# Normalizing the merged heads: four ACTIVATEs on ScalarE in place of four tensor_scalars on VectorE

## The chip, the cores and the metric

One Trainium2 chip, one core. The metric is the device time of one execution in microseconds. The profile shows the engines TensorE (PE, with its weight loads PEld), VectorE (DVE), ScalarE (ACT), GpSimd (POOL) and SyncE (SP), which here only issues transfers.

## The reference, cut to what matters

4096 tokens of width 256 go through two layers: attention in blocks, a mixture of experts, a recurrent token mixer with a channel mixer, and a second mixture of experts, each followed by a layer norm without weights. The step of this document is the first of these norms:

```python
def _layernorm(x, axis=-1, eps=1e-05):
    m = jnp.mean(x, axis=axis, keepdims=True)
    v = jnp.var(x, axis=axis, keepdims=True)
    return (x - m) / jnp.sqrt(v + eps)

x = L0_attn_hidden_states
x = _layernorm(x + _L0_attn_ref(x, ...), axis=-1)
x = _layernorm(x + _L0_ffn_ref(x, ...), axis=-1)
...
```

The attention leaves, in DRAM, the context of all 16 heads not yet divided by the sums of the softmax, and those sums. Merging the heads means: divide each head's context by its sum, add the layer's input, normalize each token's row.

## The kernel before

The program is a chain of stages, and each ends with a barrier of all engines. `merge_heads` is the third, after `project_qkv` and `attend`; `route` follows. It works on `NGRP` = 8 groups of `GRP` = 512 tokens, each as `GT` = 4 tiles of 128 rows by 256 columns, with two buffers (`s = g % 2`) for nearly everything. For a group:

- SyncE loads the contexts `c`, the sums `z` and the layer's input `hidden` (`load`, L823 to L825).
- TensorE (`bring`, L849 and L850) transposes contexts and sums of a tile into the PSUM bank `ps[j]`. It waits for all three loads of the group, and per tile for the bank.
- VectorE (`divide`, L868 and L873) takes the reciprocal of the sums and multiplies.
- GpSimd (L897) adds `hidden` and writes `x`. It waits until the group two before is normalized, whose buffer it takes.
- VectorE (`Norm.stats`, L748 and L752) takes mean and variance of each row.
- ScalarE (`Norm.root`, L761) takes the square root of the variance plus epsilon.
- VectorE (`Norm.apply`, L765 and L773) takes its reciprocal and, tile by tile, writes `y` = (x - mean) * inverse. Each tile counts up the semaphore `normed`.
- SyncE (`Norm.store`, L795) stores `y` to DRAM, once `normed` has the whole group.
- TensorE (`Norm.turn`, L783) transposes `y`, 8 blocks into two banks, and ScalarE (`Norm.copy`, L790) copies both banks to `xT`, on which `route` works.

The class `Norm` is used by two stages, `merge_heads` and `mix_channels`, each with tiles of its own name (`merge_...`, `mlp_...`). The last stage, `last_norm` (tiles `combine_...`), is code of its own: there ScalarE does the normalizing, with a scale and a bias per row.

Each engine runs its list in order, and the order within a step g is what matters here:

```python
sync:    load(g + 2)       # after added(g);   then  store(g)  after normed(g)
tensor:  bring(g + 1);     turn(g - 1)
vector:  divide(g + 1);    apply(g);    stats(g + 1)
gpsimd:  add of group g
scalar:  root(g);          copy(g - 1)
```

So the loads of group g + 3 stand behind the store of group g in SyncE's list, and the turn of group g - 1 behind the whole of `bring(g + 1)` in TensorE's.

Of the kernel before, what the change touches and what calls it, by code (L numbers as in the profile page):

```python
# [9 lines left out]
ALU = mybir.AluOpType  # L10
ACT = mybir.ActivationFunctionType
AX = mybir.AxisListType

P = 128
T = 4096
D = 256
KD = D // P
# [3 lines left out]
GT = GRP // P  # L21
# [18 lines left out]
class Mem:  # L40


    def __init__(self, nc, ctx, tag):
        self.nc, self.ctx, self.tag = nc, ctx, tag
# [18 lines left out]
def token_rows(a, g):  # L63

    return a[bass.ds(g * GRP, GRP), :].rearrange("(j p) d -> p j d", p=P)
# [640 lines left out]
def beyond(g, n):  # L706

    return not isinstance(g, int) or g > n


def skewed(first, last, step):


    for g in range(first, NGRP + last):
        step(g, g % 2)


def exists(g):

    return not isinstance(g, int) or 0 <= g < NGRP  # L720


class Norm:
# [3 lines left out]
    def __init__(self, nc, m, x, ready, out_d, ident=None, xT=None, also=()):  # L727
        self.outs = (out_d, *also)
        self.nc, self.x, self.ready, self.ident, self.xT = nc, x, ready, ident, xT
        self.y = [m.sb(f"y{i}", [P, GT, D]) for i in range(2)]  # L730
        self.part = [m.sb(f"part{i}", [P, GT, 6]) for i in range(2)]
        self.mean_var = [m.sb(f"mean_var{i}", [P, GT, 2]) for i in range(2)]
        self.std = [m.sb(f"std{i}", [P, GT]) for i in range(2)]
        self.inv = [m.sb(f"inv{i}", [P, GT]) for i in range(2)]
        self.eps = m.sb("eps", [P, 1])
        self.bank = [m.ps(f"turn{k}", [P, GRP]) for k in range(KD)] if xT is not None else None
        self.eps_set, self.parted, self.aggregated, self.std_done, self.inv_done, self.normed = (
            m.sem(a) for a in ("eps_set", "parted", "aggregated", "std_done", "inv_done", "normed"))
        self.turned, self.copied, self.passed = m.sem("turned"), m.sem("copied"), m.sem("ln_passed")
        self.stored = [m.sem(f"stored{i}") for i in range(2)]  # L740
# [22 lines left out]
    def apply(self, dve, g, s):  # L763
        dve.wait_ge(self.std_done, g + 1)
        self.nc.vector.reciprocal(self.inv[s][:, :], self.std[s][:, :]).then_inc(self.inv_done, 1)  # L765
        if beyond(g, 1):

            dve.wait_ge(self.stored[s], 16 * len(self.outs) * (g // 2))
            if self.xT is not None:
                dve.wait_ge(self.turned, KD * (g - 1))  # L770
        dve.wait_ge(self.inv_done, g + 1)
        for j in range(GT):
            self.nc.vector.tensor_scalar(self.y[s][:, j, :], self.x[g % len(self.x)][:, j, :], self.mean_var[s][:, j, 0:1],  # L773
                                         self.inv[s][:, j:j + 1], ALU.subtract, ALU.mult).then_inc(self.normed, 1)

    def turn(self, pe, g, s):
        pe.wait_ge(self.normed, GT * (g + 1))
        for k in range(KD):
            if beyond(g, 0):

                pe.wait_ge(self.copied, KD * (g - 1) + k + 1)
            for j in range(GT):
                mm = self.nc.tensor.transpose(self.bank[k][:, j * P:(j + 1) * P], self.y[s][:, j, k * P:(k + 1) * P],  # L783
                                              self.ident[:, :])
            mm.then_inc(self.turned, 1)
# [16 lines left out]
def merge_heads(nc, hs, ctx_d, sums_d, ident, out_d, xT):  # L802


    with ExitStack() as ctx:
        m = Mem(nc, ctx, "merge")
        c = [m.sb(f"c{i}", [P, KD, GRP]) for i in range(2)]
        z = [m.sb(f"z{i}", [H, GRP]) for i in range(2)]
        hidden = [m.sb(f"hidden{i}", [P, GT, D]) for i in range(2)]
        x = [m.sb(f"x{i}", [P, GT, D]) for i in range(2)]  # L810
        inv = [m.sb(f"inv_sum{i}", [P, H]) for i in range(2)]
        scaled = [m.sb(f"scaled{i}", [P, D]) for i in range(4)]
        ps = [m.ps(f"ps{i}", [P, 512]) for i in range(4)]
        in_ = [m.sem(f"in{i}") for i in range(2)]
        brought, inverted, multiplied, added = m.sem("brought"), m.sem("inverted"), m.sem("multiplied"), m.sem("added")
        norm = Norm(nc, m, x, added, out_d, ident, xT)
        block = ctx.enter_context(nc.Block())

        @block.sync
        def _(sp):  # L820
            def load(g, s):
                toks = bass.ds(g * GRP, GRP)
                sp.dma_start(c[s][:, :, :], ctx_d.rearrange("(k p) t -> p k t", p=P)[:, :, toks]).then_inc(in_[s], 16)  # L823
                sp.dma_start(z[s][:, :], sums_d[:, toks]).then_inc(in_[s], 16)
                sp.dma_start(hidden[s][:, :, :], token_rows(hs, g)).then_inc(in_[s], 16)  # L825

            def step(g, s):
                if exists(g + 2):
                    if beyond(g, -1):

                        sp.wait_ge(added, GT * (g + 1))
                    load(g + 2, s)
                if exists(g):
                    norm.store(sp, g, s)

            skewed(-2, 0, step)
            norm.finish(sp)

        @block.tensor
        def _(pe):  # L840
            def bring(g, s):
                pe.wait_ge(in_[s], 48 * (g // 2 + 1))
                for j in range(GT):
                    if beyond(g, 0):

                        pe.wait_ge(multiplied, GT * (g - 1) + j + 1)
                    cols = slice(j * P, (j + 1) * P)
                    for k in range(KD):
                        nc.tensor.transpose(ps[j][:, k * P:(k + 1) * P], c[s][:, k, cols], ident[:, :])  # L849
                    nc.tensor.transpose(ps[j][:, D:D + H], z[s][:, cols], ident[0:H, 0:H]).then_inc(brought, 1)  # L850

            def step(g, s):
                if exists(g + 1):
                    bring(g + 1, 1 - s)
                if exists(g - 1):
                    norm.turn(pe, g - 1, 1 - s)

            skewed(-1, 1, step)

        @block.vector  # L860
        def _(dve):
            norm.begin()

            def divide(g, s):
                for j in range(GT):
                    n = GT * g + j
                    dve.wait_ge(brought, n + 1)
                    nc.vector.reciprocal(inv[j % 2][:, :], ps[j][:, D:D + H]).then_inc(inverted, 1)  # L868
                    if beyond(g, 0):

                        dve.wait_ge(added, n - GT + 1)
                    dve.wait_ge(inverted, n + 1)
                    nc.vector.tensor_tensor(  # L873
                        scaled[j][:, :].rearrange("p (h d) -> p h d", h=H),
                        ps[j][:, 0:D].rearrange("p (h d) -> p h d", h=H),
                        inv[j % 2][:, :].rearrange("p (h a) -> p h a", a=1).broadcast_to([P, H, HD]),
                        ALU.mult).then_inc(multiplied, 1)

            def step(g, s):
                if exists(g + 1):  # L880
                    divide(g + 1, 1 - s)
                if exists(g):
                    norm.apply(dve, g, s)
                if exists(g + 1):
                    norm.stats(dve, g + 1, 1 - s)

            skewed(-1, 0, step)

        @block.gpsimd
        def _(pool):  # L890
            def step(g, s):
                if beyond(g, 1):

                    pool.wait_ge(norm.normed, GT * (g - 1))
                for j in range(GT):
                    pool.wait_ge(multiplied, GT * g + j + 1)
                    nc.gpsimd.tensor_tensor(x[s][:, j, :], scaled[j][:, :], hidden[s][:, j, :], ALU.add).then_inc(added, 1)  # L897

            skewed(0, 0, step)

        @block.scalar
        def _(act):
            def step(g, s):
                if exists(g):
                    norm.root(act, g, s)
                if exists(g - 1):
                    norm.copy(act, g - 1, 1 - s)

            skewed(0, 1, step)

# [1668 lines left out]
```

## Time and profile before

| | |
|---|---|
| median of 3 runs | 2062.33 us (2059.09 to 2065.66) |
| profiled execution, time | 2058.43 us |
| profiled execution, span | 2056.7 us |
| merge stage, first load to the first transfer of `route` | 661.46 to 725.86 us of the span |

The profile is of one execution. Times within it are microseconds from the start of its span. "Idle before" in a row of a timeline is how long the engine stood idle before this instruction, and what ended that. A transfer's row (SPq) is its issue; when it has landed is seen from who waited for it.

### The profile page before, as it was taken

Reading aid. Unit: us, or ns where it says so; the run is one execution under the profiler, and the core shown is the slowest. Engines: PE = TensorE matmul, PEld = TensorE weight load, DVE = VectorE, ACT = ScalarE, POOL = GpSimd, SP = SyncE. Lnnn points to the kernel's source line nnn. Section 1 sums busy time; section 2 is a strip of 40 time slices with the busy share of each in tenths; the row PEclk is TensorE's granted clock in tenths of the full one; section 3 lists DMA queues with packets and bytes.
Section 4 is the critical chain, followed back from the end, with each engine's and each line's share of the span. In section 5 each row is a group of like instructions: output and inputs, shape, how many; then the busy total and the mean of one; then the engine's idle time right before and its main releaser. Section 6 shows DMA issues by size and latency. Waiting matters only on the chain. (4 is left out here: it accounts for less than half of the span.)

```text
span 2056.7 us, 34775 instructions
## 1 busy us (share of the span) xinstructions
PE 1729.3 (84%) x12738; PEld 1378.9 (67%) x12738; DVE 1191.2 (58%) x2624; ACT 879.6 (43%) x1734; POOL 642.5 (31%) x644
## 2 busy tenths in 40 slices
PE   5859999999995778799888838969997479999991
PEld 4625766666674457767666634538997379999991
DVE  4657677777751857564443426756765755566643
ACT  2300666666675254352222216645443043444433
POOL 1340011111121467755555531113331023323111
PEclk9955799999998588899999978989999589999996
DMA  5794133333311661123333321010111322343314
GB/s 193 261 150 60 48 70 74 80 74 86 80 19 47 197 238 69 73 47 56 57 56 52 52 57 53 19 44 1 62 42 62 123 39 79 90 136 94 79 14 165
DMA packets 140644, 169.57 MB, mean 82 GB/s; under 512 B 72170, under 2 KB 108480, under 8 KB 140480
## 3 DMA queue, kind: packets, MB, share of 16 engines
q1 hardware_dynamic: 101248, 111.86, 18.5%
q0 software_dynamic: 32128, 51.82, 12.1%
q10 hardware_dynamic: 7104, 3.67, 1.3%
q8 instruction: 107, 1.75, 0.4%
q14 instruction: 57, 0.47, 0.1%
HBM read 109.20 MB, written 61.34 MB: 83 GB/s over the span
## 5 line engine op out<-in xcount | busy, mean ns | idle before, releaser
L583 DVE TENSOR_REDUCE att_neg_max<-att_m_ps 128x1 f32<-128x320 f32 x496 | 235.1, 487 | 131.4 <-PE att_m_ps L410 123.6
L410 PE MATMUL att_m_ps<-att_k,att_q 96*128 96x384 f32 x496 | 230.0, 475 | 28.4 <-DMA att_k<-qk 21.1
L1774 PE MATMUL silu_h_ps<-silu_xT,silu_w_part 128*128 128x320 f32 x1536 | 236.9, 313 | 0.9 <-DVE silu_xT L1870 0.9
L1774 PEld LDWEIGHTS silu_h_ps<-silu_xT,silu_w_part 128*128 128x128 f32 x1536 | 227.3, 189 | 2.1 <-DVE silu_xT L1870 1.3
L410 PEld LDWEIGHTS att_m_ps<-att_k,att_q 96*128 96x128 f32 x496 | 104.0, 210 | 137.3 <-DVE att_neg_max L583 87.2
L1501 POOL DMA_INDIRECT part<-gelu_y,all_table x72 | 116.3, 1616 | 135.2 <-DVE gelu_y L1621 104.0
L1739 POOL DMA_INDIRECT summed<-silu_y,all_table x40 | 63.6, 1591 | 257.1 <-DVE silu_y L1910 154.4
L548 ACT ACTIVATE att_prob_f<-att_b_ps 128x1024 f32<-128x1024 f32 x64 | 65.5, 1024 | 172.8 <-PE att_b_ps L434 172.8
L1555 PE MATMUL gelu_y_ps<-gelu_wd_high_part,gelu_hT 128*128 x512 | 109.6, 297 | 23.3 <-issue 16.6
L1786 PE MATMUL silu_y_ps<-silu_w_part,silu_h_part 128*128 128x256 f32 x960 | 117.9, 285 | 2.2 <-DVE silu_w_part L1886 2.2
L1786 PEld LDWEIGHTS silu_y_ps<-silu_w_part,silu_h_part 128*128 128x128 f32 x960 | 117.3, 194 | 2.5 <-DVE silu_w_part L1886 2.5
L1621 DVE TENSOR_SCALAR gelu_y<-gelu_y_ps,all_share 128x256 f32<-128x256 f32 x72 | 34.8, 484 | 139.9 <-DMA part<-gelu_y,all_table 121.3
L1529 PE MATMUL gelu_h_ps<-gelu_wu_part,gelu_xT 128*128 x402 | 111.5, 413 | 3.9 <-DVE gelu_wu_part L1628 2.5
L2323 PE MATMUL mlp_h_ps<-mlp_n_part,mlp_wf_part 128*128 128x512 f32 x384 | 95.9, 398 | 18.1 <-DVE mlp_n_part L2416 18.1
L1555 PEld LDWEIGHTS gelu_y_ps<-gelu_wd_high_part,gelu_hT 128*128 128x128 f32 x512 | 84.4, 192 | 36.2 <-issue 35.3
L2396 POOL TENSOR_TENSOR mlp_h_part<-mlp_squares,mlp_h_part 128x512 fp32r<-128x512 f32 x48 | 62.0, 1292 | 136.3 <-DVE mlp_h_part L2433 136.3
L1598 ACT CAST gelu_hT<-gelu_t_ps 128x512 fp32r<-128x512 f32 x64 | 37.5, 587 | 156.1 <-PE gelu_t_ps L1539 156.1
L2335 PE MATMUL mlp_y_ps<-mlp_wm_part,mlp_h_part 128*128 128x256 f32 x768 | 98.7, 286 | 3.8 <-DVE mlp_h_part L2436 3.8
L2335 PEld LDWEIGHTS mlp_y_ps<-mlp_wm_part,mlp_h_part 128*128 128x128 f32 x768 | 96.8, 194 | 7.2 <-DVE mlp_h_part L2436 5.5
L698 POOL DMA_DIRECT2D att_q<-att_max_row x8 | 4.5, 562 | 304.7 <-DVE att_max_row L604 304.7
L1882 DVE TENSOR_TENSOR silu_h<-silu_gate,silu_h_ps 128x320 f32<-128x320 f32 x128 | 62.1, 485 | 61.1 <-ACT silu_gate L1831 60.8
L586 DVE TENSOR_REDUCE att_chunk_max<-att_m_ps 128x1 f32<-128x512 f32 x128 | 87.4, 683 | 11.4 <-PE att_m_ps L414 11.1
(312 smaller groups left out, 4022.3 us busy)
## 6 DMA issues: line engine op xcount, KB each, us to landing
experts_w<-in_dram SPq DMA_DIRECT2D x24, 1024.0 KB, 8.3
qk<-qkv_part POOLq DMA_DIRECT2D x32, 512.0 KB, 3.5
att_k<-qk SPq DMA_DIRECT2D x192, 64.0 KB, 2.3
att_q<-qk SPq DMA_DIRECT2D x168, 64.0 KB, 3.1
v<-qkv_v POOLq DMA_DIRECT2D x8, 544.0 KB, 4.8
att_v<-v SPq DMA_DIRECT2D x8, 544.0 KB, 4.2
qkv_x<-in_dram SPq DMA_DIRECT2D x8, 512.0 KB, 5.7
merge_c<-context SPq DMA_DIRECT2D x8, 512.0 KB, 4.3
```

Source lines behind the costliest of these rows:

```text
L410: nc.tensor.matmul(bank[:, 0:2 * LOCAL].rearrange("p (a n) -> p a n", a=2), q[b][0:MROW, x, :], local_and_global(b, x), start=True, stop=T ...
L548: ins = nc.scalar.activation(prob_f[x][:, :, :].rearrange("p l t -> p (l t)"), b_ps[x][:, :, :, :].rearrange("p a l t -> p (a l t)"), ACT.Exp)
L583: ins = nc.vector.tensor_reduce(neg_max[p % 2][:, x:x + 1], m_ps[u % 2][:, 0:LOCAL + 2 * BLK], AX.X, ALU.max, negate=True)
L586: ins = nc.vector.tensor_reduce(chunk_max[p % 2][:, x // 8, x % 8:x % 8 + 1], m_ps[u % 2][:, :], AX.X, ALU.max)
L1501: nc.gpsimd.indirect_dma_start(out=sum_d, out_offset=bass.IndirectOffsetOnAxis(ap=table[:, 0, n:n + 1], axis=0), in_=y[n % YS][:, :], in_o ...
L1529: mm = nc.tensor.matmul(h_ps[s][:, :], a[:, k * P:(k + 1) * P], w[:, k, bass.ds(e, 1), :].rearrange("p e f -> p (e f)"), start=(i == 0), s ...
L1555: mm = nc.tensor.matmul(y_ps[s][:, :], a[:, k * P:(k + 1) * P], w[:, k, bass.ds(e, 1), :].rearrange("p e f -> p (e f)"), start=(i == 0), s ...
L1739: nc.gpsimd.indirect_dma_start(out=sum_d, out_offset=bass.IndirectOffsetOnAxis(ap=table[:, 0, n:n + 1], axis=0), in_=y[n - e * CT][:, :], ...
L1774: mm = nc.tensor.matmul(h_ps[u % 2][a][:, :], w12_part[f % RING][wp][:, a, k, :], xT[s][xp][:, k, rows], start=(i == 0), stop=(i == 3 * KD ...
L1786: mm = nc.tensor.matmul(y_ps[(s + j) % 2][:, :], h_part[hp][:, f, j * P:(j + 1) * P], w3_part[wp][:, f, :], start=(i == 0), stop=(i == 3 * ...
L2323: mm = nc.tensor.matmul(h_ps[f % 4][:, :], wf_part[wp][:, k, f * P:(f + 1) * P], n_part[g % 2][np_][:, k, :], start=(i == 0), stop=(i == 3 ...
L2335: mm = nc.tensor.matmul(y_ps[j % 2][:, :], h_part[g % 2][hp][:, f, j * P:(j + 1) * P], wm_part[wp][:, f, :], start=(i == 0), stop=(i == 3 ...
```

## The change

`Norm` gets two methods, `inverse` and `scale`, and the tiles `shift`. In `merge_heads` VectorE calls `inverse(g)` where it called `apply(g)`: the reciprocal, and shift = -mean * inverse. ScalarE calls `scale(g)` after `copy(g - 1)`: four ACTIVATEs with the function Identity, the row's inverse as scale and its shift as bias. `mix_channels` goes on calling `apply`.

```diff
--- before.py
+++ after.py
@@ -732,6 +732,8 @@
         self.mean_var = [m.sb(f"mean_var{i}", [P, GT, 2]) for i in range(2)]
         self.std = [m.sb(f"std{i}", [P, GT]) for i in range(2)]
         self.inv = [m.sb(f"inv{i}", [P, GT]) for i in range(2)]
+        self.shift = [m.sb(f"shift{i}", [P, GT]) for i in range(2)]
+        self.shift_done = m.sem("shift_done")
         self.eps = m.sb("eps", [P, 1])
         self.bank = [m.ps(f"turn{k}", [P, GRP]) for k in range(KD)] if xT is not None else None
         self.eps_set, self.parted, self.aggregated, self.std_done, self.inv_done, self.normed = (
@@ -772,6 +774,28 @@
         for j in range(GT):
             self.nc.vector.tensor_scalar(self.y[s][:, j, :], self.x[g % len(self.x)][:, j, :], self.mean_var[s][:, j, 0:1],
                                          self.inv[s][:, j:j + 1], ALU.subtract, ALU.mult).then_inc(self.normed, 1)
+
+    def inverse(self, dve, g, s):
+        dve.wait_ge(self.std_done, g + 1)
+        if g > 1:
+
+            dve.wait_ge(self.normed, GT * (g - 1))
+        self.nc.vector.reciprocal(self.inv[s][:, :], self.std[s][:, :]).then_inc(self.inv_done, 1)
+        dve.wait_ge(self.inv_done, g + 1)
+        mean = self.mean_var[s][:, :, 0:1].rearrange("p g a -> p (g a)")
+        self.nc.vector.scalar_tensor_tensor(self.shift[s][:, :], mean, -1.0, self.inv[s][:, :], ALU.mult, ALU.mult
+                                            ).then_inc(self.shift_done, 1)
+
+    def scale(self, act, g, s):
+
+        act.wait_ge(self.shift_done, g + 1)
+        if g > 1:
+
+            act.wait_ge(self.stored[s], 16 * len(self.outs) * (g // 2))
+            act.wait_ge(self.turned, KD * (g - 1))
+        for j in range(GT):
+            self.nc.scalar.activation(self.y[s][:, j, :], self.x[g % len(self.x)][:, j, :], ACT.Identity,
+                                      bias=self.shift[s][:, j:j + 1], scale=self.inv[s][:, j:j + 1]).then_inc(self.normed, 1)
 
     def turn(self, pe, g, s):
         pe.wait_ge(self.normed, GT * (g + 1))
@@ -880,7 +904,7 @@
                 if exists(g + 1):
                     divide(g + 1, 1 - s)
                 if exists(g):
-                    norm.apply(dve, g, s)
+                    norm.inverse(dve, g, s)
                 if exists(g + 1):
                     norm.stats(dve, g + 1, 1 - s)
 
@@ -905,6 +929,8 @@
                     norm.root(act, g, s)
                 if exists(g - 1):
                     norm.copy(act, g - 1, 1 - s)
+                if exists(g):
+                    norm.scale(act, g, s)
 
             skewed(0, 1, step)
 
```

## Rows read from the trace of the kernel before

**Rows 1.** Page: the span, and each engine's busy time, share and instructions.

```profile
span 2056.7 us, 34775 instructions
...
PE 1729.3 (84%) x12738; PEld 1378.9 (67%) x12738; DVE 1191.2 (58%) x2624; ACT 879.6 (43%) x1734; POOL 642.5 (31%) x644
```

**Rows 2.** Windows, merge stage: length, then busy time of PE, PEld, DVE, ACT, POOL.

```profile
669.00:724.00 55.00, 40.02 (x152) 26.04 (x153) 46.74 (x166) 11.67 (x24) 22.54 (x32) 0.50 0.59 192
```

**Rows 3.** Waits of SyncE's queue: total us, times, longest.

```profile
SPq L795 <- DVE merge_y L773: 37.5, 8, 6.3
```

**Rows 4.** Timeline, one period: start us, length, engine, line, operation [idle before].

```profile
692.03 0.34 SPq L795 DMA_DIRECT2D rows<-merge_y  x1
...
692.46 0.69 PE L849 MATMUL merge_ps<-all_ident,merge_c 128*128 128x128 f32 x2 [1.31 <-DMA merge_hidden<-in_dram]
...
693.08 0.28 PE L850 MATMUL merge_ps<-all_ident,merge_z 16*128 16x16 f32 x1
...
693.76 0.23 DVE L868 RECIPROCAL merge_inv_sum<-merge_ps 128x16 f32<-128x16 f32 x1
...
694.66 2.83 POOL L897 TENSOR_TENSOR merge_x<-merge_scaled,merge_hidden 128x256 f32<-128x256 f32 x4 [3.77 <-DVE merge_scaled L873]
...
695.58 0.28 PE L850 MATMUL merge_ps<-all_ident,merge_z 16*128 16x16 f32 x1
...
695.79 1.97 PE L783 MATMUL merge_turn<-all_ident,merge_y 128*128 128x128 f32 x8
...
696.60 0.17 DVE L765 RECIPROCAL merge_inv<-merge_std 128x4 f32<-128x4 f32 x1
...
696.91 1.70 DVE L773 TENSOR_SCALAR merge_y<-merge_x,merge_mean_var,merge_inv 128x256 f32<-128x256 f32 x4
...
697.80 0.58 ACT L790 COPY turned_xT<-merge_turn 128x512 f32<-128x512 f32 x1 [0.27 <-PE merge_turn L783]
...
698.53 1.39 DVE L748 BATCH_NORM_STATS2 merge_part<-merge_x 128x6 f32<-128x256 f32 x4
698.64 0.34 SPq L795 DMA_DIRECT2D rows<-merge_y  x1
...
699.10 0.69 PE L849 MATMUL merge_ps<-all_ident,merge_c 128*128 128x128 f32 x2 [1.34 <-DMA merge_hidden<-in_dram]
...
705.99 0.69 PE L849 MATMUL merge_ps<-all_ident,merge_c 128*128 128x128 f32 x2 [1.59 <-DMA merge_hidden<-in_dram]
```

**Rows 5.** Timeline, the first groups of the stage.

```profile
672.25 0.36 SPq L823 DMA_DIRECT2D merge_c<-context  x1
...
676.87 0.17 DVE L765 RECIPROCAL merge_inv<-merge_std 128x4 f32<-128x4 f32 x1
...
678.28 0.69 PE L849 MATMUL merge_ps<-all_ident,merge_c 128*128 128x128 f32 x2 [3.94 <-DMA merge_hidden<-in_dram]
...
678.90 0.34 SPq L795 DMA_DIRECT2D rows<-merge_y  x1
...
685.85 0.69 PE L849 MATMUL merge_ps<-all_ident,merge_c 128*128 128x128 f32 x2 [2.27 <-DMA merge_hidden<-in_dram]
```

**Rows 6.** Timeline, end of the stage and start of routing.

```profile
712.17 10.94 SPq L795 DMA_DIRECT2D rows<-merge_y  x3
...
722.82 1.97 PE L783 MATMUL merge_turn<-all_ident,merge_y 128*128 128x128 f32 x8 [1.98 <-DVE merge_y L773]
...
725.86 0.38 SPq L1080 DMA_DIRECT2D route_wg<-in_dram  x1
```

**Rows 7.** Timeline of `last_norm`, its first group.

```profile
2036.18 0.16 DVE L958 SCALAR_TENSOR_TENSOR combine_shift<-combine_mean_var,combine_inv 128x4 f32<-128x4 f32 x1
...
2036.37 2.07 ACT L984 ACTIVATE combine_out<-combine_x,combine_shift,combine_inv 128x256 f32<-128x256 f32 x4 [0.21 <-DVE combine_shift L958]
```

**Rows 8.** Groups by line on ScalarE, of `last_norm`: count, busy us, mean ns.

```profile
L984 ACT ACTIVATE combine_out<-combine_x,combine_shift,combine_inv 128x256 f32<-128x256 f32 x32 | 16.4, 584 | 0.2 <-DVE combine_shift L958 0.2
...
L975 ACT ACT_TABLE_LOAD x1 | 1.3, 1283 | 36.0 <-DVE combine_mean_var L952 36.0
```

## The prediction

> **What bounds the kernel now.** I read the page first. Over the whole span VectorE is busy 58%, ScalarE 43% and TensorE 84% [rows 1]; such shares average over stages that have nothing to do with one another, so the next view is the windows of the merge stage alone. There VectorE is busy 46.74 of 55 us (85%) and ScalarE 11.67 (21%) [rows 2]. At this point the change looks like a plain gain: work leaves the fullest engine for one that is four fifths idle.
>
> The waits of SyncE's queue say otherwise. The store of the normalized rows waits for L773 eight times, 37.5 us in all [rows 3]. In the code the three loads of group g+3 stand behind the store of group g in that queue. So the next loads go out when normalizing ends, and the question is whether those loads are late. The timeline of one period answers it. I write T(g) for the start of `bring(g)` and S(g) for the issue of the store of group g. S(2) = 692.03 sends the loads of group 5 off, and T(5) = 699.10, with TensorE idle until `merge_hidden` has landed: 7.07 us from store to landing. T(4) = 692.46, and S(3) = 698.64: 6.18 us from landing to store [rows 4]. The two make a closed loop over two groups: T(g+1) to S(g) to T(g+3) takes 6.18 + 7.07 = 13.25 us, or 6.62 us a group. From S(2) to S(3) the trace has 6.61. So the loop through the load accounts for the whole pace. VectorE is nearly as full, but not ahead of it: the first tile of `bring(4)` is there at 693.08 + 0.28 = 693.36 and VectorE takes it at 693.76, 0.40 later [rows 4].
>
> **What the change does to the loop, part by part.** All times below are counted from T(g+1).
>
> VectorE loses four `tensor_scalar` per group (from 696.91 to 698.53, 1.62 us with their overlap [rows 4]) and gets one small `scalar_tensor_tensor`, 0.16 us in `last_norm` [rows 7]. It still waits on its own reciprocal: in the present code 0.31 us from 696.60 to 696.91 [rows 4], and I take the same for the new one. VectorE's relief is about 1.4 us per group, and none of it is on the loop by itself: VectorE then idles until the loads land.
>
> The moved work is four ACTIVATEs with scale and bias from SBUF, the same shapes as `last_norm`'s L984: four in 2.07 us, starting 0.19 us after the start of the shift's instruction [rows 7]. Alone one is 584 ns [rows 8]; four without any overlap would be 2.34 us, which is the upper bound. The lower bound is the 1.62 us that VectorE needs; I take 2.07 since it is the same operation on the same engine.
>
> What decides is where they stand in ScalarE's queue: behind `copy(g - 1)`. That copy waits for `turn(g - 1)`, and TensorE does that turn only after the whole of `bring(g + 1)`. From the rows: `bring(4)` starts at 692.46, the turn at 695.79 (3.33 later), and the second copy ends at 697.80 + 0.58 = 698.38, 5.92 after T [rows 4]. Today this tail runs beside VectorE's normalizing and nobody waits for it. In the changed order `scale(g)` cannot start before 5.92.
>
> Is the shift there by then? The last tile of `bring(4)` is ready at 695.58 + 0.28 = 695.86, 3.40 after T [rows 4]. VectorE, now waiting for tiles, takes it then; dividing one tile takes about 0.7 us ((696.60 − 693.76)/4 = 0.71), the reciprocal and its wait 0.31, and from the shift to ScalarE's start 0.19: 4.6 us. So the copies end last, by 1.3 us, and their wait takes the place of VectorE's slot.
>
> S(g) then comes at 5.92 + 2.07 = 7.99 after T(g+1) in place of 6.18 (the small hop to SyncE, some 0.1 us, is about what back-to-back ACTIVATEs overlap by, 0.584 − 2.07/4 = 0.07). The loop becomes 7.99 + 7.07 = 15.06, or 7.53 us a group.
>
> The other edits cost nothing, with their cover: ScalarE's square root of group g stands behind `scale(g - 1)`, long before the shift is wanted; the added waits on `stored` and `turned` are for transfers and turns of two groups earlier; GpSimd's add of group g waits for normalizing of g-2, which by this loop ends 7.9 after T(g-1), a little after T(g), while its own first input needs 1.7 us after T(g) or more. If that last cover were gone, each microsecond would only move the statistics, which have over 2 us of idle VectorE behind them. The semaphore and the two small tiles cost no instruction in the loop.
>
> **The sum.** Walk through the even groups, which set the end, with 7.07 from store to landing (the rows have 685.85 − 678.90 = 6.95 for the first and 705.99 − 698.64 = 7.35 at most [rows 4, 5]). Group 0 has no copy ahead of it: reciprocal at 676.87 as now, shift at +0.31, ScalarE at +0.19, then 2.07 and 0.1 for the hop give S(0) = 679.54 (now 678.90). T(3) = 679.54 + 6.95 = 686.49. S(2) = T(3) + 7.99 = 694.48. T(5) = 701.55, S(4) = 709.54, T(7) = 716.61, S(6) = 724.60. The odd groups stay ahead: S(1) = T(2) + 7.99 = 678.28 + 7.99 = 686.27, T(4) = 693.34, S(3) = 701.33, T(6) = 708.40, S(5) = 716.39.
>
> The tail has no load to wait for, but the same order: `turn(6)` starts at S(6), its copies end 695.79 to 698.38 = 2.59 later [rows 4], at 727.19, and `scale(7)` ends 2.07 later. S(7) = 729.26. Now the last turn starts at 722.82, and the third of the last three stores ends at 712.17 + 10.94 = 723.11, so S(7) is at 722.8 too [rows 6]. The stage ends with this store's landing, since routing starts only after it, at 725.86 [rows 6]. That step is the same in both, so routing and all behind it shifts by 729.26 − 722.8 = +6.4 us. Bounds: 2.34 in place of 2.07 in the five slots S(0), S(2), S(4), S(6), S(7) adds 1.3; 7.35 in place of 7.07 for two landings and of 6.95 for the first adds 1.0; 6.95 everywhere takes 0.2. So +6.2 to +8.7 us within this picture, the middle of the durations at +6.4.
>
> The profiled execution took 2058.43 us, so its sum is 2064.8. The median of the runs, 2062.33, lies 3.9 above it, and I carry the difference over: 2068.7 us, 0.31% longer.
>
> **A rule against the trace.** The rows of the merge stage name VectorE as its fullest engine, 46.74 of 55 us [rows 2]. The Trainium skill (Perfetto Trace Analysis, Identifying the Most-Contended Engine) says to optimize the engine with the highest occupancy first; by that rule this change is well aimed and the time would fall, as in the first rival below. The trace has the gap that limits on another engine, TensorE's idle before `bring`, so I don't follow it here.
>
> **Rivals.**
> First, faster: VectorE is the bound and the loads are not. Its slot shrinks by 1.4 us, until the statistics meet GpSimd: its add ends at 694.66 + 2.83 = 697.49 and the statistics start at 698.53 today [rows 4], so 1.0 us a group could go, 7.0 over seven: 2055.3. For it speaks VectorE's 85%; against it that T(g+3) hangs on S(g) by the order of the queue, and S(g) now on the copies. It decides if `scale` could start before 4.1 after T.
>
> Second, the operation's price alone: if the copies were out of the way, `scale` would start at 4.6 and S(g) come at 6.7 after T, 0.5 later than now (6.18). The 0.64 of S(0), 0.5 at S(2), S(4) and S(6), and 2.07 against 1.62 in the tail make 0.64 + 1.5 + 0.45 = 2.6 us: 2064.9, which is within 0.3%. It needs the copies to end 1.3 us earlier than the rows have them. The Trainium skill (ScalarE: Activation LUTs, Rules for kernel authors) would have multiplies and adds on VectorE rather than ScalarE; that speaks against the change by the same price, 0.45 us a group, which the rows bear out.
>
> Third, landings get quicker with more room. Today a store and the next loads follow one another closely. The loads of group 2, with no store ahead of them, took 678.28 − 672.25 = 6.03 [rows 5]; if three landings came 0.7 sooner, +6.4 becomes +4.3: 2066.6, within 0.3%. Against it: store and loads still leave as one burst.
>
> Fourth, much slower: square root and Identity want different tables. Two loads of 1.28 us a group, one of them ahead of `scale`, add 5 x 1.28 = 6.4: 2075.1. `last_norm` alternates the same two with one load for 32 ACTIVATEs [rows 8], so this is unlikely.
>
> **How the numbers follow.** A difference under 0.3%, some 6 us, can hardly be told from none here. The forecast has 0.70, the rivals 0.05, 0.08, 0.13 and 0.04. The forecast's own value sits just above that limit; 0.48 of its 0.70 falls above and 0.22 below. So slower 0.48 + 0.04 = 0.52, same 0.22 + 0.08 + 0.13 = 0.43, faster 0.05. The range: below, it takes in the second and third rivals and the 3 us by which a single run of the kernel strays; above, the forecast's upper bound (+8.7, 2071.0) and the same scatter: 2062.5 to 2074.
>
> **What would show it.** In the profile after: L773 gone from this stage and four ACTIVATEs of about 2.07 us in its place, starting right behind the second copy and not behind the shift; VectorE idle before L868, waiting for TensorE; stores some 7.5 us apart on average instead of 6.6; 7.0 to 7.1 us from each store to the next landing; the last store near 729 and routing near 732. The prediction is wrong if `scale` starts on the shift, if the landings change by more than half a microsecond, if a table is loaded within the stage, or if the stage after gives the delay back.

## The result and the profile after

Twenty runs of the changed kernel have a median of 2067.07 us (2063.47 to 2072.64), twenty of the kernel before 2059.11 us (2051.84 to 2070.92). The two medians lie 7.96 us apart. The ratio of the two sets of runs is 1.0036, with a 95% interval from 1.0024 to 1.0048: the change costs 0.36%, or 7.4 us (4.9 to 9.9). Forecast were 2068.7 us and +6.4 us, 0.31%. The profiled execution took 2063.47 us.

The page of the changed kernel, the same rows as [rows 1]:

```profile
span 2061.4 us, 34789 instructions
...
PE 1728.9 (84%) x12738; PEld 1377.4 (67%) x12738; DVE 1184.2 (57%) x2600; ACT 895.4 (43%) x1766; POOL 642.9 (31%) x644
```

VectorE has lost 24 instructions and 7 us, ScalarE has gained 32 instructions and 16 us, and the span is 4.7 us longer. The merge stage alone, in the same window as [rows 2]:

```profile
669.00:724.00 55.00, 36.21 (x137) 23.04 (x137) 39.25 (x139) 23.76 (x49) 22.26 (x32) 0.50 0.55 176
```

VectorE fell from 46.74 to 39.25 us of 55 and ScalarE rose from 11.67 to 23.76: the work moved as intended. TensorE did less in the same time, 36.21 in place of 40.02. The last three numbers of the row are TensorE's granted clock as a share of full speed (0.50, that is 1.2 of 2.4 GHz, as before), the busy share of the DMA engines (0.55, before 0.59) and the GB/s that they moved. The wait of SyncE's queue for the normalized rows, the row that answers to [rows 3]:

```profile
SPq L819 <- ACT merge_y L797: 43.9, 8, 8.6
```

Again all eight stores wait, now for ScalarE, and 43.9 us in place of 37.5: 6.4 us more. The timeline of one period, to be read beside [rows 4]. (L873 is `bring`, L807 the turn, L814 the copies, L783 and L786 reciprocal and shift, L797 the four ACTIVATEs, L819 the store.)

```profile
692.15 0.69 PE L873 MATMUL merge_ps<-all_ident,merge_c 128*128 128x128 f32 x2 [0.63 <-DMA merge_hidden<-in_dram]
...
694.14 0.34 SPq L819 DMA_DIRECT2D rows<-merge_y  x1
...
694.19 3.00 POOL L921 TENSOR_TENSOR merge_x<-merge_scaled,merge_hidden 128x256 f32<-128x256 f32 x4 [2.94 <-ACT merge_y L797]
...
695.49 1.97 PE L807 MATMUL merge_turn<-all_ident,merge_y 128*128 128x128 f32 x8
...
696.30 0.17 DVE L783 RECIPROCAL merge_inv<-merge_std 128x4 f32<-128x4 f32 x1
...
696.50 0.71 DVE L786 SCALAR_TENSOR_TENSOR merge_shift<-merge_mean_var,merge_inv 128x4 f32<-128x4 f32 x1
...
697.49 0.58 ACT L814 COPY turned_xT<-merge_turn 128x512 f32<-128x512 f32 x1 [0.27 <-PE merge_turn L807]
...
697.97 2.08 ACT L797 ACTIVATE merge_y<-merge_x,merge_shift,merge_inv 128x256 f32<-128x256 f32 x4
...
700.07 0.34 SPq L819 DMA_DIRECT2D rows<-merge_y  x1
...
701.05 0.69 PE L873 MATMUL merge_ps<-all_ident,merge_c 128*128 128x128 f32 x2 [3.60 <-DMA merge_hidden<-in_dram]
...
707.04 0.69 PE L873 MATMUL merge_ps<-all_ident,merge_c 128*128 128x128 f32 x2 [0.69 <-DMA merge_hidden<-in_dram]
```

`bring(4)` starts at 692.15. Its last transposes are followed by the turn of group 2 at 695.49 (+3.34), the second copy ends at 697.49 + 0.58 = 698.07 (+5.92), and the ACTIVATEs start on its heels at 697.97, the back-to-back overlap of 0.1 included. The shift was there at 696.50 + 0.71 = 697.21, 0.76 earlier. The store comes at 700.07: 7.92 us after `bring(4)` started, where it was 6.18. From S(2) = 694.14 to T(5) = 701.05 it is 6.91 us, and from S(3) = 700.07 to T(6) = 707.04 it is 6.97. The start and the end of the stage, beside [rows 5] and [rows 6]:

```profile
666.64 0.69 PE L873 MATMUL merge_ps<-all_ident,merge_c 128*128 128x128 f32 x2 [22.29 <-DMA merge_hidden<-in_dram]
...
673.64 1.28 ACT L763 ACT_TABLE_LOAD   x1 [30.45 <-DVE merge_mean_var L754]
...
676.44 0.70 DVE L786 SCALAR_TENSOR_TENSOR merge_shift<-merge_mean_var,merge_inv 128x4 f32<-128x4 f32 x1
...
677.18 2.07 ACT L797 ACTIVATE merge_y<-merge_x,merge_shift,merge_inv 128x256 f32<-128x256 f32 x4 [1.94 <-DVE merge_shift L786]
...
679.28 0.34 SPq L819 DMA_DIRECT2D rows<-merge_y  x1
...
686.22 0.69 PE L873 MATMUL merge_ps<-all_ident,merge_c 128*128 128x128 f32 x2 [3.46 <-DMA merge_hidden<-in_dram]
...
714.97 13.91 SPq L819 DMA_DIRECT2D rows<-merge_y  x3
...
724.35 0.16 DVE L786 SCALAR_TENSOR_TENSOR merge_shift<-merge_mean_var,merge_inv 128x4 f32<-128x4 f32 x1
...
731.62 0.38 SPq L1106 DMA_DIRECT2D route_wg<-in_dram  x1
```

The first `bring` of the kernel before:

```profile
667.26 0.69 PE L849 MATMUL merge_ps<-all_ident,merge_c 128*128 128x128 f32 x2 [20.99 <-DMA merge_hidden<-in_dram]
```

The first store comes 12.64 us after the first `bring` (666.64 to 679.28); before it came 678.90 − 667.26 = 11.64 after it. The landing takes 686.22 − 679.28 = 6.94. The last store is issued at 728.56 (the row of three stores ends at 714.97 + 13.91 = 728.88, and this issue takes 0.32), and routing starts at 731.62. From the first `bring` to routing the stage takes 64.98 us; before it took 725.86 − 667.26 = 58.60. The difference is 6.38 us, and forecast were 6.4.

I count the stage from the first `bring`, because what lies outside it strays by several microseconds from one profiled execution to the next: between the issue of the first load and the first `bring` lie 5.80 us before, 7.10 after, and 6.2 to 7.5 in the runs below, all but one of which have the same code there; from routing to the end of the span 1330.84 before, 1329.78 after, and 1325.0 to 1334.7 below.

### The profile page after: what moved, and what is told of

Same layout as the page of the kernel before. It is cut to its first block and busy times, and to the rows that moved or that the text cites. A ratio compares the mean times of both kernels' runs of the same rounds, so it can differ in the third digit from the quotient of the medians.

```text
span 2061.4 us, 34789 instructions
## 1 busy us (share of the span) xinstructions
PE 1728.9 (84%) x12738; PEld 1377.4 (67%) x12738; DVE 1184.2 (57%) x2600; ACT 895.4 (43%) x1766; POOL 642.9 (31%) x644
## 3 DMA queue, kind: packets, MB, share of 16 engines
q10 hardware_dynamic: 7104, 3.67, 1.1%
## 5 line engine op out<-in xcount | busy, mean ns | idle before, releaser
L558 ACT ACTIVATE att_prob_b<-att_b_ps 128x512 f32<-128x512 f32 (+1 forms) x128 | 74.5, 582 | 45.4 <-PE att_b_ps L455 41.5
```

What stands on the lines that cost most here:

```text
L558: nc.scalar.activation(prob_b[x][:, :, own, :], b_ps[x][:, :, own, :], ACT.Exp)
```

## The experiments

The theory, as in the prediction: the pace is set by a loop from landing to store and from store to landing, and the change lengthens it, because ScalarE's ACTIVATEs stand behind the copies of the group before. The rivals: it is the operation on ScalarE that costs; VectorE was the bound; or the transfers' bandwidth sets the pace.

A stage time is from one profiled execution of each kernel. How much it varies from one execution to the next was not measured; the timed ratios, of 11 to 20 runs, stand beside it.

| kernel | stage, first bring to routing, us | against before, us | ratio, timed (95%) |
|---|---|---|---|
| before | 667.26 to 725.86: 58.60 | | |
| the change | 666.64 to 731.62: 64.98 | +6.38 | 1.0036 (1.0024 to 1.0048) |
| ACTIVATEs ahead of the copies | 669.48 to 732.06: 62.58 | +3.98 | 1.0031 (1.0021 to 1.0041) |
| the change, late store | 668.86 to 725.06: 56.20 | −2.40 | 0.9997 (0.9984 to 1.0010) |
| before, late store | 669.56 to 727.84: 58.28 | −0.32 | 0.9998 (0.9987 to 1.0009) |
| late store and ACTIVATEs ahead | 670.42 to 725.05: 54.63 | −3.97 | 0.9981 (0.9968 to 0.9994) |
| these two and a third buffer | 666.91 to 720.30: 53.39 | −5.21 | 0.9975 (0.9959 to 0.9990) |
| before, VectorE behind the copies | 668.80 to 731.29: 62.49 | +3.89 | 1.0024 (1.0007 to 1.0041) |
| the change, adds on VectorE | 667.76 to 736.21: 68.45 | +9.85 | not timed |

By the timed runs the change, the ACTIVATEs ahead and VectorE behind the copies are slower than before, and the kernels with both edits and with the third buffer are faster. The two kernels with the late store alone can't be told from before, nor from one another.

### The ACTIVATEs ahead of the copies

```diff
 def step(g, s):          # scalar
     if exists(g):
         norm.root(act, g, s)
-    if exists(g - 1):
-        norm.copy(act, g - 1, 1 - s)
     if exists(g):
         norm.scale(act, g, s)
+    if exists(g - 1):
+        norm.copy(act, g - 1, 1 - s)
```

> Theory (the loop through the load, with the copies of the group before ahead of the four ACTIVATEs): with the ACTIVATEs ahead of the copies, the normalizing starts on the shift, about 5.1 us after bring(g+1) starts (in the profile of the changed kernel 697.22 for the 692.15), in place of 5.8. So the store comes some 7.2 us after it in place of 7.92, three times 0.7 less, and in the tail S(6) to S(7) is about 2.9 us in place of 4.6: 3.8 us less than the changed kernel, some 2.6 us more than before (ratio to before 1.001). Rival (the cost is the ACTIVATEs themselves, or the shift's instruction, 0.70 to 0.76 us instead of 0.16): the order does not matter, store to store stays at 7.47 us on average, ratio to before 1.003 to 1.004.

The timeline around the normalizing of group 2:

```profile
689.25 0.69 PE L873 MATMUL merge_ps<-all_ident,merge_c 128*128 128x128 f32 x2 [3.73 <-DMA merge_hidden<-in_dram]
...
693.60 0.70 DVE L786 SCALAR_TENSOR_TENSOR merge_shift<-merge_mean_var,merge_inv 128x4 f32<-128x4 f32 x1
...
694.33 2.07 ACT L797 ACTIVATE merge_y<-merge_x,merge_shift,merge_inv 128x256 f32<-128x256 f32 x4 [5.54 <-DVE merge_shift L786]
...
696.43 0.34 SPq L819 DMA_DIRECT2D rows<-merge_y  x1
...
703.10 0.69 PE L873 MATMUL merge_ps<-all_ident,merge_c 128*128 128x128 f32 x2 [3.29 <-DMA merge_hidden<-in_dram]
...
732.06 0.38 SPq L1106 DMA_DIRECT2D route_wg<-in_dram  x1
```

The ACTIVATEs now start on the shift (693.60 + 0.70 = 694.30, start 694.33), 5.08 us after `bring(3)`, and the store comes 696.43 − 689.25 = 7.18 after it, as the theory has it (7.2). The landing takes 6.67. The stage is 2.40 us shorter than with the change and not 3.8. Half of what is missing is an oversight: `copy(5)` now stands between `scale(6)` and the square root of the last group, so from S(6) to S(7) it takes 3.67 us in place of 4.62, and 2.9 had been expected. The other half is the last store's landing, 3.3 us in this profile and 2.6 in that of the change; why it took longer stays open. The order matters, so the rival that only the operation costs is out for this part. But the price without the copies is still 1.00 us a period (7.18 against 6.18), where the prediction's second rival had 0.5: the shift's instruction, now on the path, takes 0.70 and not 0.16. The timed ratio, 1.0031, is higher than the stage alone would make it (3.98 of 2059 us is 1.0019, just below its interval; why is open); the timed runs can't separate this kernel from the change, and I rest the reading on the stage.

### The store one step later

```diff
                     load(g + 2, s)
-                if exists(g):
-                    norm.store(sp, g, s)
+                if exists(g - 1):
+                    norm.store(sp, g - 1, 1 - s)

-            skewed(-2, 0, step)
+            skewed(-2, 1, step)
             norm.finish(sp)
```

This one edit was made to the changed kernel and to the kernel before.

> The changed kernel, with the store of a group put one step later in SyncE's list, so that the loads of group g+3 no longer stand behind the store of group g. Theory (the loop through store and load sets the pace): the loads go out when GpSimd has added group g+1, about 4.8 us after bring(g+1), and land some 6.5 us later; 11.3 us for two groups, so TensorE starts a bring every 5.7 to 6.0 us in place of 7.5, though nothing about ScalarE's order or work is changed. The last store comes about 9 us earlier than in the changed kernel, 3 us earlier than before (ratio to before 0.9985). Rival (ScalarE's work, its wait for the copies, or the transfers' bandwidth sets the pace): bring to bring stays above 7 us, ratio 1.003 or so.

> The kernel before, with the same late store. Theory (VectorE and the loop bound the kernel before to the same 6.6 us a group): with the loop opened VectorE still needs 2.84 + 0.31 + 1.62 + 1.54 + 0.29 = 6.6 us a group, so the stage gains 1 us at most: ratio 0.9995 to 1.000. Rival (the loop alone bounds it, VectorE has room): the gain is as large as in the changed kernel with the late store, 3 us or more, ratio 0.9985 or less.

The changed kernel with the late store, issues of SyncE and starts of `bring`:

```profile
684.94 0.36 SPq L847 DMA_DIRECT2D merge_c<-context  x1
...
687.62 0.34 SPq L819 DMA_DIRECT2D rows<-merge_y  x1
...
691.40 0.36 SPq L847 DMA_DIRECT2D merge_c<-context  x1
...
697.51 0.69 PE L873 MATMUL merge_ps<-all_ident,merge_c 128*128 128x128 f32 x2 [0.51 <-DMA merge_hidden<-in_dram]
...
703.68 0.69 PE L873 MATMUL merge_ps<-all_ident,merge_c 128*128 128x128 f32 x2 [0.86 <-DMA merge_hidden<-in_dram]
...
709.46 0.69 PE L873 MATMUL merge_ps<-all_ident,merge_c 128*128 128x128 f32 x2 [0.48 <-DMA merge_hidden<-in_dram]
...
725.06 0.38 SPq L1106 DMA_DIRECT2D route_wg<-in_dram  x1
```

The loads now go out ahead of the store (684.94 and 687.62), and `bring` follows `bring` in 6.17 and 5.78 us, in place of 7.45 (half of 692.15 to 707.04 above). ScalarE's order and work are those of the change. The stage lost 8.78 us, and 9 were expected. So the loop through SyncE's queue is what the change had lengthened: with ScalarE's order and work as they are, the stage runs at some 6 us a group once the loads no longer wait for them, and the transfers can go faster than they did. The wait for the copies is then still worth something, 1.57 us, as the kernel with both edits shows.

The kernel before with the same edit, its stores:

```profile
681.45 0.50 SPq L795 DMA_DIRECT2D rows<-merge_y  x1
...
688.00 0.50 SPq L795 DMA_DIRECT2D rows<-merge_y  x1
...
694.54 0.50 SPq L795 DMA_DIRECT2D rows<-merge_y  x1
...
701.09 0.50 SPq L795 DMA_DIRECT2D rows<-merge_y  x1
...
708.00 17.09 SPq L795 DMA_DIRECT2D rows<-merge_y  x4
```

They are 6.55, 6.54, 6.55 and 6.91 us apart, as before the edit (6.61 in [rows 4]), and the stage gains 0.32 us. The view of this kernel's waits (total us, times, longest) has one wait of VectorE for a tile from TensorE in the whole stage, the one for the first tile:

```profile
DVE merge_inv_sum L868 <- PE merge_ps L850: 7.9, 1, 7.9
```

So here VectorE is the bound, at the same pace at which the loop had been. That is the part of the first rival that was true: VectorE's relief is worth something, 58.28 − 56.20 = 2.08 us, but only where the loop is open. This rests on the two stages; the timed ratios, 0.9998 and 0.9997, don't show it.

### Both edits, and a third buffer

> The changed kernel with the late store and with the ACTIVATEs ahead of the copies. Theory: the loads set the pace as with the late store alone (5.7 to 6.0 us a group), and the order on ScalarE takes 0.7 us off the last group but one and 1.7 off the tail: some 5.5 us less than before, ratio 0.9973, the fastest of all. Rival (the order is worth nothing once the loop is open): the same as with the late store alone.

The stage is 1.57 us shorter than with the late store alone, where 2.4 were expected: with the same oversight the tail from S(6) to S(7) fell by 0.95 us and not by 1.7, and routing follows the last store 0.35 us later. The kernel is faster than before, 0.9981, and its median lies under those of both single edits. The next kernel adds a third buffer for `c`, `z` and `hidden`, so that a load needs no longer wait for the adds of the group two before:

```diff
-        c = [m.sb(f"c{i}", [P, KD, GRP]) for i in range(2)]
+        c = [m.sb(f"c{i}", [P, KD, GRP]) for i in range(3)]
...
-                if exists(g + 2):
+                if exists(g + 3):
...
-                    load(g + 2, s)
+                    load(g + 3, g % 3)
...
-            skewed(-2, 1, step)
+            skewed(-3, 1, step)
```

> Late store, ACTIVATEs ahead of the copies, and a third buffer for the three loads, so that the loads of group g+3 wait for the adds of group g and not of group g+1. Theory (with late store and order changed, the loads still set the pace at 5.98 us a group, and VectorE with GpSimd needs 5.5, as the first three groups there show: the shifts at 680.23, 685.74, 691.30): TensorE no longer waits for a landing, 5.5 to 5.6 us a group, 2 to 2.5 us less than with the two changes alone; ratio to before 0.997. Rival (the transfers' bandwidth is the limit): 6.0 us a group, nothing gained.

```profile
679.56 0.34 SPq L819 DMA_DIRECT2D rows<-merge_y  x1
...
685.12 0.34 SPq L819 DMA_DIRECT2D rows<-merge_y  x1
...
690.67 0.34 SPq L819 DMA_DIRECT2D rows<-merge_y  x1
...
696.24 20.96 SPq L819 DMA_DIRECT2D rows<-merge_y  x5
...
720.30 0.38 SPq L1106 DMA_DIRECT2D route_wg<-in_dram  x1
```

The first stores are 5.56, 5.55 and 5.57 us apart, the pace that was expected of VectorE and GpSimd; from S(0) to S(6) it is 5.61 on average. The gain is 1.24 us and not 2 to 2.5, since with the two edits the stores had been 5.82 us apart on average (683.07 to 717.97 for six groups) and not 5.98. Bandwidth is no limit at 5.55 us a group. This is the fastest kernel here, 0.9975, though by the intervals it can't be told from the one with the two edits.

### VectorE behind the copies

The kernel before, with the position of the change and without its operation; `behind` is set for `merge_heads` alone.

```diff
         dve.wait_ge(self.inv_done, g + 1)
+        if self.xT is not None and self.behind and g > 0:
+            dve.wait_ge(self.copied, KD * g)
         for j in range(GT):
             self.nc.vector.tensor_scalar(self.y[s][:, j, :], ...
```

> The kernel before, VectorE normalizing as ever, but the four tensor_scalars of group g held back until ScalarE has copied group g-1: the position of the change without its operation. Theory (the position behind the copies is most of the price): the store comes 5.92 + 0.1 + 1.4 to 1.6 + 0.1 = 7.5 to 7.7 us after bring(g+1) in place of 6.2, the first store is unchanged, and the stage from the first bring to routing is about 3.8 us longer than before (62.4 in place of 58.60); ratio 1.002. The remaining 2.6 us of the change are then the operation (2.07 against 1.62 or less) and the first group's 0.6. Rival (the price is ScalarE's operation, the position is free): as before, 58.6 us, ratio 1.000.

```profile
687.34 0.69 PE L852 MATMUL merge_ps<-all_ident,merge_c 128*128 128x128 f32 x2 [2.35 <-DMA merge_hidden<-in_dram]
...
692.68 0.59 ACT L793 COPY turned_xT<-merge_turn 128x512 f32<-128x512 f32 x1 [0.27 <-PE merge_turn L786]
...
693.40 1.38 DVE L776 TENSOR_SCALAR merge_y<-merge_x,merge_mean_var,merge_inv 128x256 f32<-128x256 f32 x4 [1.63 <-ACT turned_xT L793]
...
694.82 0.34 SPq L798 DMA_DIRECT2D rows<-merge_y  x1
...
731.29 0.38 SPq L1083 DMA_DIRECT2D route_wg<-in_dram  x1
```

The second copy ends at 693.27, VectorE starts at 693.40, and the store comes 694.82 − 687.34 = 7.48 us after `bring(3)` (7.5 to 7.7 were expected). The stage is 62.49 us long, expected were 62.4. So the position costs 3.89 us by itself, with VectorE's operation. The remaining 2.49 of the 6.38 us are nearly all ScalarE's operation: the first store 1.00 later, and three times 7.92 against 7.48. The split depends on the order in which the two are taken. Moved behind the copies, the four tensor_scalars took 1.38 us, where they had taken 1.70 in [rows 4], because GpSimd's add was over by then (see the last section); and taking the position out of the change, with the ACTIVATEs ahead of the copies, gave back 2.40 and not 3.89.

### GpSimd idle

In the changed kernel the adds are moved into VectorE's `divide`, and GpSimd's list, whose removal is left out below, is empty.

```diff
+                    if g > 1:
+                        dve.wait_ge(norm.normed, GT * (g - 1))
+                    dve.wait_ge(multiplied, n + 1)
+                    nc.vector.tensor_tensor(x[s][:, j, :], scaled[j][:, :], hidden[s][:, j, :], ALU.add).then_inc(added, 1)
```

> The changed kernel with the adding of the layer's input moved from GpSimd to VectorE, so that GpSimd does nothing in the stage; only the duration of the shift's instruction is of interest. Theory (the instruction waits for GpSimd's running add, with which its end coincides): 0.16 to 0.23 us in all eight groups, in place of 0.70 to 0.76 in seven of eight. Rival (it is slow for another reason, such as ScalarE's or TensorE's reading at the same time): 0.70 to 0.76 again. VectorE gets 1.6 to 1.8 us more work a group, so the stage may be longer.

The shift's instruction in this kernel, from the view of its tile (count, then shortest, median and longest in ns, first and last start):

```profile
L786 DVE SCALAR_TENSOR_TENSOR merge_shift<-merge_mean_var,merge_inv x8: 161/162/164, 679.8 to 728.9; 128x4 f32<-128x4 f32 x8
```

and in the changed kernel:

```profile
L786 DVE SCALAR_TENSOR_TENSOR merge_shift<-merge_mean_var,merge_inv x8: 161/708/756, 676.4 to 724.3; 128x4 f32<-128x4 f32 x8
```

Eight times 161 to 164 ns with GpSimd idle, against a median of 708 with GpSimd adding. In this kernel the last shift runs beside TensorE's turn (728.93 within 728.55 to 730.52) and isn't stretched; in the changed kernel the first one is stretched, at 676.44, while ScalarE is idle until 677.18. So neither of those two is the cause. The stage is longer, 68.45 us, as VectorE now has the adds as well.

## Why the prediction was right

**What bounds the stage.** Right that the loop of 6.18 + 7.07 bounds the kernel before, and that the change lengthens it; too strong in that VectorE is "not ahead of it". The row given for that, the first tile ready at 693.36 and taken at 693.76, says the opposite: the tile waited for VectorE. Only at the fourth tile, ready at 695.86, has VectorE caught up, and takes it 0.04 later (a row of the same period of the kernel before):

```profile
695.90 0.26 DVE L868 RECIPROCAL merge_inv_sum<-merge_ps 128x16 f32<-128x16 f32 x1
```

Before, both bounds ran at the same pace. The late store shows both sides: the changed kernel gains 8.78 us from opening the loop, the kernel before 0.32, since VectorE's own list takes as long there. It didn't hurt the forecast, because the change relieves VectorE and lengthens the loop.

**The position behind the copies.** Right: the copies end at +5.92 in both kernels, and the ACTIVATEs start there. Holding VectorE back to the same place costs 3.89 us by itself.

**The operation.** 2.07 us were forecast from `last_norm`, and 2.07 or 2.08 were measured. T to S is 7.92 against 7.99. The 1.62 us of VectorE, taken as what it needs, held a wait of some 0.33 for GpSimd: in the last group, with no add running, its four take 1.38.

**Landings.** 6.94, 6.91 and 7.05 us in the even groups, a little less than the 6.95, 7.07 and 7.07 of the sum. The third rival had this sign, but 0.2 us in all where it needed 2.1: it does not hold.

**The shift.** Here a term was mis-sized: 0.16 us, taken from `last_norm`, where GpSimd has nothing to do. In seven of eight groups it took 0.70 to 0.76. From group 1 on it cost nothing, because the copies were later still: the room was 0.76 us and not 1.3. In group 0 no copy stands ahead, and it cost 0.54 us: the ACTIVATEs start at 677.18 on the shift's end at 677.14, and the first store comes 12.64 us after the first `bring`, where the sum had 679.54 − 667.26 = 12.28. With the ACTIVATEs ahead of the copies it is on the path in every group but the last.

**The tail and the sum.** S(7) was put 729.26 − 667.26 = 62.00 us behind the first `bring`; it came 728.56 − 666.64 = 61.92 behind it. That this fits to 0.1 us is luck: the first store came 0.36 later than summed, and the landings (0.19), the three slots (0.07 each) and the tail (0.04) together 0.44 earlier. Of the terms costed at nothing, the cover of GpSimd's add had gone: the first product of group 4 is there at 693.90 and the add starts at 694.19, released by the ACTIVATEs of group 2. These 0.3 us moved nothing, since the fourth product, at 696.38, holds the last add anyway. No table was loaded for Identity: ScalarE's one load in the stage, at 673.64, is ahead of the first square root, as it was before.

**The rivals.** VectorE as the sole bound is refuted by the result and by the late store, though its relief is real; the Trainium skill's advice to work on the engine with the highest occupancy (Perfetto Trace Analysis, Identifying the Most-Contended Engine) agrees with the trace only after the loop has been opened, by 2.08 us. The operation's price alone is refuted by VectorE behind the copies; and that price was put too low, at 2.6 us, since with the ACTIVATEs ahead the stage is 3.98 longer than before, 0.7 of it the late landing of the last store. The absolute time was only 1.6 us off, and that is luck in part: it was built on a median 3.2 us above that of all twenty runs of the kernel before, and the difference was 1.0 us too small, within its interval.

## What to carry to other kernels

Before moving work to an idle engine, find who waits for its result and what stands ahead of it in that engine's list: an idle engine can still have the late item first. A store that shares a queue with the next loads makes the loads wait for whatever the store waits for; here one step of delay for the store took more from the stage (8.78 us) than the move had added (6.38). Where two bounds run at the same pace, lifting one alone shows little: opening the loop alone gave 0.32 us. Relieving VectorE with nothing else changed was not tried.

## What the hardware showed that was not expected

A `scalar_tensor_tensor` on 128x4 elements took 0.16 us with GpSimd idle and 0.70 to 0.76 us while GpSimd was in one of its adds, and it ended with that add: in the period above, 696.50 + 0.71 = 697.21, and the four adds 694.19 + 3.00 = 697.19. In all seven stretched groups the two ends lie within 0.03 us of one another. The reciprocal just before it, 0.17 us, ran beside the add unhindered. In the last group, with no add left, it took 0.16 (the row of 724.35). The Trainium skill (SBUF — State Buffer, Who interferes with whom) says that VectorE and GpSimd share a pair of ports to SBUF, which is an exclusive lock, and that a VectorE instruction with two inputs in SBUF contends with a GpSimd instruction that reads SBUF; the trace agrees, and so does the run with GpSimd idle (0.161 to 0.164 us eight times).

The kernel before had shown the same kind of wait (count, then shortest, median and longest in ns, first and last start):

```profile
L773 DVE TENSOR_SCALAR merge_y<-merge_x,merge_mean_var,merge_inv x32: 400/402/878, 677.1 to 722.4; 128x256 f32<-128x256 f32 x32
```

In each of the seven groups in which GpSimd was adding, the first of the four tensor_scalars took 0.73 to 0.88 us and ended 0.14 to 0.16 after the add; the others, and all four of the last group, took 0.40 or 0.41.
